# A perceiver kernel on one core: the order of the local attention slot, three buffers of turned probabilities, and the banks in which the tokens are turned

## What is computed

```python
def attn_layer(x, Wqkv, qs, ksc, Wo):          # 16 heads of 64 channels
    q, k, v = split(x @ Wqkv)
    q = l2norm(q) * qs;  k = l2norm(k) * ksc
    q = q * cos * scale + rotate_half(q) * sin * scale
    k = k * cos / scale + rotate_half(k) * sin / scale
    out = softmax(mask(8 * q @ k.T)) @ v        # windows of 64, each sees itself and the one before
    return out @ Wo

def ffn_layer(x, g, bln, W1, b1, W2, b2):
    xn = (x - mean) / sqrt(var + 1e-5) * g + bln
    a, gate = split(xn @ W1 + b1)
    return a * gelu(gate) @ W2 + b2

for i in range(6):                              # shift_tokens moves half the channels by one token
    x = attn_layer(shift_tokens(x), ...) + x
    x = ffn_layer(shift_tokens(x), ...) + x
```

## Time and profile before

| | us |
|---|---|
| median of three runs | 2145.43 (2145.41 to 2150.28) |
| the profiled execution, own time | 2145.24 |
| its span | 2143.4 |
| PE busy | 2040.7 (95%) |
| DVE busy | 1723.7 (80%) |
| ACT busy | 1392.7 (65%) |

### The profile page before, as it was taken

One profiled execution on the slowest core, in us unless ns is written; L12 is line 12 of the kernel. 1 busy time (PEld: TensorE's weight loads), 2 busy tenths in 40 slices (PEclk: granted clock), 3 DMA queues, 4 the chain that ended last, 5 costly groups with the idle time before them and its releaser, 6 DMA issues.

```text
span 2143.4 us, 51804 instructions
## 1 busy us (share of the span) xinstructions
PE 2040.7 (95%) x17400; PEld 1704.1 (80%) x17400; DVE 1723.7 (80%) x4874; ACT 1392.7 (65%) x4026; POOL 550.3 (26%) x317
## 2 busy tenths in 40 slices
PE   5999999999998998999999999999999999999988
PEld 4787887887886676888888888888888888888877
DVE  6786787787676498898889888898889888988883
ACT  3776567567564355676767676866777676767653
POOL 2111111111111334232323233232323242323220
PEclk9999999999999999999999999999999999999999
DMA  3000000000000410021102011201120111011010
GB/s 120 8 10 1 7 12 1 7 12 1 6 26 0 140 31 15 13 72 33 56 14 72 14 58 31 72 14 46 44 73 14 34 57 52 25 33 55 14 33 20
DMA packets 50017, 72.10 MB, mean 34 GB/s; under 512 B 9429, under 2 KB 36869, under 8 KB 49541
## 3 DMA queue, kind: packets, MB, share of 16 engines
q1 hardware_dynamic: 47429, 64.30, 9.9%
q10 hardware_dynamic: 2368, 4.98, 0.6%
HBM read 51.58 MB, written 2.10 MB: 25 GB/s over the span
## 4 chain that ended last, share of the span: by engine, by line
PE 47%; issue 7%; DVE 4%; DMA 3%; ACT 3%; POOL 2%; SPq 1%; DVEq 0%; ACTq 0%; POOLq 0%
PE ps_loc L1722 17%; PE ps_loc L1830 7%; PE ps_loc L1799 5%; PE ps_loc L1761 4%; PE ps_loc L1841 4%; PE ps_loc L1772 4%; DMA late<-y_all 3%; PE ps_loc L1741 3%; PE ps_loc L1788 3%; POOL rnorm L2655 2%; PE ps_loc L1342 1%; ACT xnT_high L2077 1%; ACT pT L2060 1%; ACT xnT_loc L2077 1%; DVE w_low L2259 0%
## 5 line engine op out<-in xcount | busy, mean ns | idle before, releaser
L2655 POOL TENSOR_TENSOR rnorm<-norm_floor,half_loc 128x32 f32<-128x32 f32 x48 | 300.5, 6261 | 582.7 <-DVE norm_floor L2270 385.2
L1722 PE MATMUL ps_loc<-w_high,xT 128*128 128x512 f32 x1152 | 379.3, 410 | 0.7 <-ACT qk L2032 0.6
L2053 ACT ACTIVATE prob_loc<-prob_loc,top_loc 128x128 f32<-128x128 f32 x768 | 299.2, 402 | 45.2 <-DVE top_loc L2334 43.2
L718 ACT ACTIVATE prob<-prob,new_top 128x256 f32<-128x256 f32 x512 | 252.2, 497 | 0.0
L1722 PEld LDWEIGHTS ps_loc<-w_high,xT 128*128 128x128 f32 x1152 | 203.9, 189 | 51.4 <-issue 9.3
L2334 DVE CUSTOM_DVE_ANT_0 prob_loc<-ps_loc,const,rnorm 128x128 f32<-128x128 f32 x768 | 218.8, 345 | 28.0 <-PE ps_loc L1761 25.8
L1722 PE MATMUL ps_loc<-w_low,xT 128*128 128x512 f32 x576 | 228.5, 397 | 0.0
L2045 ACT ACTIVATE qT_loc<-ps_loc 128x512 f32<-128x512 f32 x96 | 57.4, 598 | 238.1 <-PE ps_loc L1741 238.1
L923 DVE CUSTOM_DVE_ANT_0 prob<-ps_cross,bias 128x256 f32<-128x256 f32 x512 | 184.7, 420 | 20.7 <-PE ps_cross L494 11.1
L1799 PE MATMUL ps_loc<-wo,qT_loc 128*128 128x256 f32 x768 | 169.8, 379 | 1.3 <-ACT qT_loc L2067 1.3
L1179 POOL TENSOR_TENSOR o<-o,alpha 128x1024 f32<-128x1024 f32 x32 | 61.0, 1906 | 425.1 <-DVE o L962 333.4
(11 more groups left out here) (214 smaller groups left out, 4869.0 us busy)
## 6 DMA issues: line engine op xcount, KB each, us to landing
w_raw<-in_ffn_Wqkv_dram SPq DMA_DIRECT2D x24, 512.0 KB, 5.7
w_raw<-in_ffn_Wqkv_dram SPq DMA_DIRECT2D x24, 256.0 KB, 3.9
wo<-in_ffn_Wo_dram SPq DMA_DIRECT2D x24, 256.0 KB, 3.5
v_mid<-v_even SPq DMA_DIRECT2D x24, 256.0 KB, 3.4
v_mid<-v_odd SPq DMA_DIRECT2D x24, 256.0 KB, 3.7
w<-in_ffn_W_dram SPq DMA_DIRECT2D x12, 341.0 KB, 3.3
w<-in_ffn_W_dram SPq DMA_DIRECT2D x6, 640.0 KB, 4.6
ctx_raw<-in_ctx_dram SPq DMA_DIRECT2D x12, 256.0 KB, 2.8
```

The costliest lines, as they stand in the source:

```text
L718: ins = act.activation(prob[:, t, h, :], prob[:, t, h, :], ACT.Exp, bias=new_top[:, t, h:h + 1], scale=-1.0, accum_out=chunk_sum[:, t, h:h ...
L1722: ins = pe.matmul(ps[:, DENSE + j % 2, :], xT[:, px, kk, t * P:(t + 1) * P], wqkv[pw][:, kk, col:col + 512], start=kk == 0 and n == 0, sto ...
L2053: ins = act.activation(pr, pr, ACT.Exp, bias=top[:, h, t:t + 1], scale=-1.0, accum_out=total[:, h, t:t + 1])
L2655: pool.tensor_tensor(rnorm[:, b % 2, t, :], norm2_floor[:, :], half[:, :], ALU.pow).then_inc(rnorm_done, 8)
```

## The change

On PE, `turn_xn` now writes bank 4 and `turn_x` bank 5, which belong to the scores, instead of banks 0 and 1; they wait for `minima` of pair 5 instead of for copies of projections. `pT` has three buffers instead of two. `turn_xn` moves ahead of `project(11)`, and `turn_probs(4)` ahead of `out(1)`. On ACT a one-element exponential comes after `q_out`, `qkv_out(0)` goes ahead of `exps(0)`, `exps(7)` moves up to follow `o_out(0)`, `xn_out` is split in `xn_high`, ahead of `qkv_out(11)`, and `xn_copy`, behind `probs_out(4)`. `widen(0)` starts after `xn_high` alone. On DVE, `share(0)` comes ahead of `moments`, `share(1)` ahead of `normal`, shares 3 to 6 come earlier, `sums(n, 0)` later, and `o_out(1)` comes ahead of `x_low`. The making of weight pieces moves too: `weights_high(0)` from ahead of `probs_out(4)` to behind `probs_out(6)`, `weights_low(0)` from ahead of `x_low` to behind `gated(0)`. The squares are on ACT before and after.

```diff
+    TURNED = 3
-        pT = sb("pT", [P, 2, 2, TT, P])
+        pT = sb("pT", [P, TURNED, 2, TT, P])
+        XN_TURN, X_TURN, FIRST_X = 4, 5, DENSE + 1
...
@@ tensor: helpers
-                pe.wait_ge(qkv_done, a)
+                    bank = X_TURN
+                    pe.wait_ge(s_read, now + 2 * RING)
...
-            def turn_xn(a, ahead):
-                pe.wait_ge(xn_done, a + U)
-                if ahead:
-                    pe.wait_ge(qkv_done, a + 2 * U + SLOTS - 1)
-                pe.wait_ge(u_done, a)
+            def turn_xn(f, a):
+                pe.wait_ge(xn_done, f + U)
+                pe.wait_ge(s_read, a + 2 * RING)
...
-                    pe.wait_ge(xnT_copied, a + U)
-                if m == 1 and turn:
-                    pe.wait_ge(xT_done, a + 4 * U)
+                    pe.wait_ge(xnT_copied, a + U // 2)
+                if m < 2:
+                    pe.wait_ge(u_done, a)
+                if m < 2 and ahead:
+                    pe.wait_ge(qkv_done, a + 2 * U + (SLOTS - 1 if m == 0 else U))
@@ tensor: slot
                 turn_probs(a, 3)
+                if ffn:
+                    turn_xn(f, a)
                 if ahead:
                     project(n, nb, 11)
-                if ffn:
-                    turn_xn(f, ahead)
+                turn_probs(a, 4)
                 out(a, L, b, 1)
-                turn_probs(a, 4)
@@ scalar
-                act.wait_ge(o_full, a + 4 * (pair // 2))
+                act.wait_ge(o_full, a + (4 * ((pair - TURNED) // 2 + 1) if pair >= TURNED else 0))
...
                 q_out(a)
-                exps(a, 0)
+                act.activation(exp_warm[:, :], zero[:, :], ACT.Exp)
                 if ahead:
                     qkv_out(n, nb, 0)
+                exps(a, 0)
...
                 o_out(a, 0)
+                exps(a, 7)
                 if ahead:
                     qkv_out(n, nb, 10)
                 probs_out(a, 3)
+                if ffn:
+                    xn_high(f, L if b else L - LAYER, fb)
                 if ahead:
                     qkv_out(n, nb, 11)
+                probs_out(a, 4)
                 if ffn:
-                    xn_out(f, L if b else L - LAYER, fb)
-                if split:
-                    weights_high(L + LAYER, 0)
-                probs_out(a, 4)
+                    xn_copy()
                 if turn:
                     x_out(L + U * (b + 2))
-                exps(a, 7)
                 probs_out(a, 5)
-                if split:
-                    weights_high(L + LAYER, 1)
                 if ffn:
                     gates(f, 0)
                 probs_out(a, 6)
+                if split:
+                    weights_high(L + LAYER, 0)
                 if ffn:
                     gates(f, 1)
                 if split:
+                    weights_high(L + LAYER, 1)
                     weights_high(L + LAYER, 2)
@@ vector
                 minima(a, b, 1)
+                minima(a, b, 2)
+                inverse(a, 0)
+                share(a, 0)
                 if ffn:
                     moments(f, fb, shifts)
-                inverse(a, 0)
-                share(a, 0)
...
+                share(a, 6)
                 if ffn:
                     xn_low(f)
-                if split:
-                    weights_low(L + LAYER, 0)
+                o_out(a, 1)
                 if turn:
                     x_low(L + U * (b + 2))
                 inverse(a, 7)
-                o_out(a, 1)
-                share(a, 6)
+                share(a, 7)
+                if ffn:
+                    gated(f, 0)
+                if split:
+                    weights_low(L + LAYER, 0)
+                if ahead:
+                    sums(n, 0)
+                o_out(a, 2)
+                if ffn:
+                    gated(f, 1)
                 if split:
                     weights_low(L + LAYER, 1)
-                if ffn:
-                    gated(f, 0)
-                o_out(a, 2)
-                share(a, 7)
-                if ffn:
-                    gated(f, 1)
```

108 lines of the change are left out of this document (59 added, 49 removed).

## The result

| | before | after |
|---|---|---|
| median, us | 2145.42 (2143.09 to 2150.28) | 2168.82 (2167.76 to 2175.95) |
| span of the profiled execution, us | 2143.4 | 2168.0 |

The ratio is 1.0113, with a 95% interval of 1.0085 to 1.0141: the change makes the kernel 1.1% slower. Slower was forecast, but the time lies above the range of 2143 to 2166. The two spans differ by 24.6 us where 11.0 were forecast.

What follows compares the result with a forecast made beforehand. PE was taken to bound the kernel, busy 95% of the span. Terms of -3.3 - 0.4 - 4.6 + 20.5 - 1.3 + 0.1 = +11.0 us on 2145.24 gave 2156 us, range 2143 to 2166.

Steps and rivals of the forecast that it cites:

- Third slots: Five third slots: PE waits 3.6 us before widen(3) for gated(1), queued behind weights_low(0); 56.5 to 60.6 us each, +20.5.
- half clock: PE matmuls behind the third slots' new wait: 1.2 GHz instead of 2.4 for 3.4 us, 1.1 us more per slot.
- Plain slots: PE's 0.63 us wait before turn_probs(5) moves to xnT_low in widen(0); a slot gains 0.06 us, to 55.29.
- Fourth slots: Five fourth slots: earlier qkv_out(0) and share(0) remove PE's waits; 56.33 to 55.4 us each, -4.6 in all.
- Second and first slots: share(0) ahead of moments ends PE's wait before turn_probs(0): second slots -3.3 us; first slots and first layer's second -0.4.
- The last slot and the tail: Last two slots and tail: exps(7) ahead of probs_out(3), widen(0) after half the copies; +0.1 us, between -2 and +2.
- The banks: PE's turn_xn and turn_x in new PSUM banks: worth nothing, since no listed PE wait was for bank 0 or 1.

Runs made afterwards that it cites:

- run 2: The kernel after the change, with weights_low(0) moved on DVE from ahead of sums to behind gated(1): 2155.95 us, ratio 1.0043.
- run 6: The kernel before, with only the change's new places for the weight pieces on ACT and DVE: 2151.82 us, ratio 1.0034.
- run 1: The kernel after the change, with the two waits in gates exchanged, f_full first and u_done second: 2160.88 us, ratio 1.0078.
- run 9: The kernel before, with early shares, qkv_out(0) ahead of exps(0), the one-element exponential, and each weight piece of third slots one place later: 2140.28 us, ratio 0.9974.
- run 7: The kernel before, with DVE's early minima(2) and shares, ACT's one-element exponential and qkv_out(0) ahead of exps(0): 2140.44 us, ratio 0.9973.
- run 8: The kernel before, with the two waits in gates exchanged: 2144.56 us, ratio 0.9993.
- run 10: The kernel before, with DVE's new order alone (minima(2), share(0) ahead of moments, share(1) ahead of normal): 2141.71 us, ratio 0.9985.
- run 11: The kernel after, with the two waits in gates exchanged and exps(7) of the last slot back behind probs_out(3): 2157.7 us, ratio 1.0065.

## Why the prediction was wrong, step by step

**Third slots: right.** Forecast +20.5, measured +21.15, with the wait, its place and its queue. It foresaw 59.5 us if the clock holds and 60.6 with half clock; the one slot of the five at full clock takes 59.51, the others 60.4 to 61.8. The two conditions are shown by runs 2 and 6. Two things in it were not as said. DVE waits 1.91 us for the piece where some 3 were said, because `gated(0)` came 1.08 us late; in run 1, where it doesn't, the wait is 3.00 and PE's is 3.35 as before. And the half clock, for which one length was taken, came in three of them: none, about 3 us and about 7 us. That its mean cost fits is in part luck.

**Plain slots: right.** The wait moved to `xnT_low`, and the slot lasts 55.4 where 55.29 was said. In the slot from 1064.45:

```profile
1096.92 0.51 PE L1841 MATMUL ps_loc<-xnT_low,w_high 128*128 128x256 f32 x2 [0.33 <-DVE xnT_low L2420]
```

PE idles 0.33 us instead of 0.63, yet nothing is won: from the start of `widen(0)` to `out(2)` PE takes 3.60 us (1095.88 to 1099.48) instead of the 3.02 of the kernel before (and of run 9, which has the old order there). This wait in the midst of a group costs 0.58, of which the profile shows 0.33 as idle.

**Fourth slots: the step that failed.** "I take them at 55.4" rested on the gain at the slot's start, and that gain is real: 3.2 us over five slots in run 7. What was not asked is what `sums`, now between `gated(0)` and `gated(1)`, does when no piece is there. Its 2.2 us have room only if the first gate is in time, and in these slots it comes 1.1 us late, behind a load that waits for `widen(0)`. The walk through the slot was made with one where the load doesn't wait, from 1060.92, and carried over to slots where it does. The wait stood in the program before too, where it cost nothing (run 8). That is +5.0 of the 6.45 us between forecast and measurement; the rest is a gain taken too large (3.2 where 4.6 was said).

**Second and first slots: the same step.** The forecast -3.3 for second slots was of the right size, 2.8 by runs 7 and 10. In the last layer, whose slots are all of the form with the waiting load, one second, one first and one third slot lost 1.0 us each again (run 1 gives them back). Without this one step the time would have come into the range: run 1 has all of the change but the order of the two waits, and its 2160.9 us lie between 2143 and 2166.

**The last slot and the tail: too small, and for the most part open.** +0.1 was said, for the third slot of the last layer too, between -2 and +2, and +4.15 measured. 1.1 of it is that third slot, by the waiting load. The other 3.0 are in the last slot, whose length is not the same from profile to profile. Here it is in the kernel before, the kernel after and runs 1, 6 and 8, with PE's busy time behind the length and the granted clock third from the end:

```profile
2069.12:2143.40 74.28, 57.54 (x515) 50.80 (x513) 35.31 (x128) 32.31 (x100) 5.81 (x7) 0.91 0.10 31
2090.68:2168.00 77.32, 62.41 (x515) 55.28 (x513) 35.58 (x128) 32.40 (x101) 5.50 (x7) 0.82 0.09 30
2083.34:2159.00 75.66, 58.86 (x515) 52.22 (x513) 35.59 (x128) 32.41 (x101) 5.50 (x7) 0.89 0.10 31
2073.92:2147.30 73.38, 55.42 (x515) 49.17 (x513) 35.30 (x128) 32.19 (x100) 5.81 (x7) 0.95 0.10 32
2067.39:2145.10 77.71, 60.17 (x515) 53.60 (x513) 35.29 (x128) 32.18 (x100) 5.79 (x7) 0.85 0.09 30
```

Runs 6 and 8 have the last slot of the kernel before (run 8 with the gate's two waits exchanged), and it lasts 73.4 us at a clock of 0.95 in one and 77.7 us at 0.85 in the other. From before to after, PE stands still 1.8 us less in it (14.9 for 16.7), but is busy for 4.9 us more with as many matmuls, at 0.82 instead of 0.91. So the 3.0 us came with the clock and not with longer waits. Whether the change brings the lower clock about, or one profile of each happened to show it, stays open, and with it what runs 1 and 11 seem to win there (1.7 and 0.7 us).

**The banks: right, as far as it goes.** They were said to bring nothing. The Trainium skill, "Perfetto Trace Analysis", under Optimizing Tensor Performance, wants independent matmul groups to rotate through different PSUM banks. By the rows, after the change no plain slot is shorter than before: 277.2 us for five first slots in run 1, which has the new banks, against 276.84 in the earlier trace rows. Neither the banks nor the third buffer of `pT` were tried alone.
